# Latent projection in one piece, even maxima turned behind it, one softmax exponential and the value copies behind a group's exponentials, six steps moved

## What is computed

```python
# causal self-attention, 32 query heads, 8 key heads, head width 16
q = (x @ wq).reshape(b, s, NH, HD); k = (x @ wk)...; v = (x @ wv)...
attn = softmax(where(causal, q k^T * HD**-0.5, min))     # 56 x 56 for a head
x = x + (attn v) @ wo
# cross-attention over 1500 context rows, in a latent space of 32
C_q = Q @ Wq_d                                   # Q = layernorm(x)
C_kv = K @ Wkv_d                                 # the latents: 1500 x 32 for an element
scores = (C_q @ W_qk) C_kv^T / sqrt(LKV)         # 16 heads x 56 rows x 1500
out = softmax(scores) @ (C_kv @ Wv_u)
x = x + out
# feed-forward with a LoRA term
x = x + layernorm(x) @ kernel + bias + LoRA
```

## Time and profile before

| | |
|---|---|
| median of 3 executions | 644.15 us |
| profiled execution, its own time | 645.84 us |
| its span, first to last instruction | 644.0 us |
| PE matmul busy | 584.1 us, 91% |
| DVE busy | 432.5 us, 67% |
| POOL busy | 412.7 us, 64% |
| ACT busy | 302.1 us, 47% |
| granted TensorE clock, mean | 0.968 |

### The profile page before, as it was taken

The page is one execution under the profiler, slowest core; times in us unless marked ns, Lnnn a source line. Parts: engine busy times, 40 slices in busy tenths (PEclk is TensorE's granted clock), DMA queues, the critical chain, the costliest instruction groups (busy, mean ns, idle before and its releaser), DMA issues.

```text
span 644.0 us, 11508 instructions
## 1 busy us (share of the span) xinstructions
PE 584.1 (91%) x4164; PEld 315.5 (49%) x4164; DVE 432.5 (67%) x715; ACT 302.1 (47%) x642; POOL 412.7 (64%) x385
## 2 busy tenths in 40 slices
PE   7889797998999899999999899998999899988887
PEld 7436353455446354545446355455446355434445
DVE  2737964678757967778747957678757967656632
ACT  1421434537444555437444555437444555464460
POOL 5002166598758887598758887588758887789000
PEclk9997788899999999999999999999999999999899
DMA  9959511651048110751039110761039110200000
GB/s 320 409 107 348 208 36 24 251 206 35 12 120 317 59 45 22 268 204 39 9 108 336 52 45 22 253 219 32 16 93 334 68 45 23 64 19 0 24 2 15
DMA packets 31578, 77.40 MB, mean 120 GB/s; under 512 B 11297, under 2 KB 24961, under 8 KB 29218
## 3 DMA queue, kind: packets, MB, share of 16 engines
q1 hardware_dynamic: 30854, 75.27, 34.9%
q10 hardware_dynamic: 668, 1.40, 0.6%
HBM read 58.92 MB, written 2.88 MB: 96 GB/s over the span
## 4 chain that ended last, share of the span: by engine, by line
PE 58%; DVE 19%; ACT 6%; POOL 4%; SPq 4%; issue 4%; DMA 4%; ACTq 0%; POOLq 0%; DVEq 0%
PE st_ps L711 11%; PE mx_ps L754 9%; PE pv_ps L726 8%; PE mi_ps L496 4%; PE mi_ps L490 4%; DVE mx_p L1143 4%; POOL acc L1214 3%; PE mi_ps L503 3%; DVE p L1066 2%; PE mi_ps L586 2%; SPq L402 2%; DMA ctx_sb<-in_ctx_t 2%; DVE xn L1018 2%; PE mi_ps L590 2%; DVE p L1107 2%
## 5 line engine op out<-in xcount | busy, mean ns | idle before, releaser
L1214 POOL TENSOR_TENSOR acc<-acc,p_ring 125x448 f32<-125x448 f32 x290 | 348.0, 1200 | 65.4 <-ACT p_ring L941 25.8
L1143 DVE TENSOR_REDUCE mx_p<-mx_ps 128x1 f32<-128x500 f32 x336 | 210.0, 669 | 98.9 <-PE mx_ps L754 97.9
L941 ACT ACTIVATE p_ring<-st_ps 125x448 f32<-125x448 f32 x372 | 183.4, 544 | 151.6 <-PE st_ps L711 139.7
L711 PE MATMUL st_ps<-q_st,c_st 98*125 98x448 f32 x372 | 146.3, 432 | 9.8 <-ACT p_ring L941 8.6
L754 PE MATMUL mx_ps<-c_st,q_st 96*128 96x500 f32 x336 | 142.1, 457 | 12.2 <-DVE mx_p L1143 5.1
L711 PEld LDWEIGHTS st_ps<-q_st,c_st 98*125 98x125 f32 x372 | 65.3, 190 | 99.3 <-ACT p_ring L941 79.9
L726 PE MATMUL pv_ps<-p_ring,c_nat 125*32 125x448 f32 x768 | 94.5, 564 | 1.9 <-ACT ox L840 1.0
L754 PEld LDWEIGHTS mx_ps<-c_st,q_st 96*128 96x128 f32 x336 | 63.6, 197 | 43.7 <-DVE mx_p L1143 17.6
L1222 POOL TENSOR_TENSOR rstd<-mv,eps_col 128x1 f32<-128x1 f32 x24 | 4.6, 190 | 117.1 <-DVE mv L1014 116.6
L503 PE MATMUL mi_ps<-ctx_sb,wkv_sb 128*32 128x375 f32 x480 | 46.8, 511 | 5.5 <-DVE p L1066 5.5
L1214 POOL TENSOR_TENSOR acc<-p_ring 125x448 f32<-125x448 f32 x29 | 35.6, 1226 | 19.2 <-ACT p_ring L941 19.2
(11 more groups left out here) (137 smaller groups left out, 677.9 us busy)
## 6 DMA issues: line engine op xcount, KB each, us to landing
ctx_sb<-in_ctx_t SPq DMA_DIRECT2D x16, 3000.0 KB, 11.6
c_st<-ct_hl SPq DMA_DIRECT2D x192, 46.9 KB, 2.3
q_st<-q_hl SPq DMA_DIRECT2D x90, 56.0 KB, 2.0
x_sb<-in_x SPq DMA_DIRECT2D x8, 256.0 KB, 2.8
out_y<-x3n SPq DMA_DIRECT2D x16, 112.0 KB
wq_sb<-in_wq SPq DMA_DIRECT2D x2, 512.0 KB, 6.4
kern_sb<-in_lora_a SPq DMA_DIRECT2D x1, 1024.0 KB, 14.2
wo_sb<-in_wo SPq DMA_DIRECT2D x1, 1024.0 KB, 17.6
```

Source lines behind the costliest of these rows:

```text
L711: mm(st_bank(unit)[0:KC, 0:HALF], c_st[:, b % 4, t * KT + k * KC:t * KT + (k + 1) * KC], q_st[:, b // 2 % 2, b % 2, half * HALF:(half + 1) ...
L941: act.activation(p_ring[:, unit % PR, :], st_bank(unit)[0:KC, 0:HALF], ACT.Exp, scale=float(L) ** -0.5).then_inc(exp_done, 1)
L1143: ve.tensor_reduce(mx_p[:, p:p + 1], mx_ps[unit % MXB][:, 0:KP], AX.X, ALU.max).then_inc(red_done, 1)
L1214: po.tensor_tensor(dst, first, p_ring[:, unit % PR, :].rearrange("p (h s) -> p h s", s=S), ALU.add).then_inc(acc_done, 1)
```

## The change

```diff
-PIECES_IN = [3, 2, 4, 0, 0, 0, 0, 3, 4, 0, 3, 0]
+PIECES_IN = [3, 2, 4, 0, 0, 0, 0, 3, 4, 0, 2, 0]
-FIRST_PIECES_IN = [3, 2, 4, 0, 0, 0, 2, 4, 4, 0, 0, 0]
+FIRST_PIECES_IN = [3, 2, 4, 0, 0, 0, 1, 4, 4, 0, 0, 0]

 STEPS = [
-    [("Ah", "a"), ("M", 2), ("L0", "n"), ("M", 1), ("A", "a"), ("AS", "a"), ("N0", "n")],
+    [("L0", "n"), ("Ah", "a"), ("A", "a"), ("M", 2), ("N0", "n"), ("M", 1), ("AS", "a")],
     [("CT", "a"), ("M", 1), ("T1", "n")],
     [("K", "n"), ("M", 1), ("Qh", "n"), ("M", 3), ("Q1", "n")],
-    [("WA", "n"), ("M", 1), ("SA", "n"), ("M", 2), ("WB", "n"), ("M", 1), ("NM", "m"), ("SB", "n"), ("SM0", "n"),
+    [("WA", "n"), ("M", 2), ("SA", "n"), ("M", 1), ("WB", "n"), ("M", 1), ("SB", "n"), ("NM", "m"), ("SM0", "n"),
      ("SM1", "n")],
-    [("SE0", "n"), ("Ah", "b"), ("MT", "m"), ("A", "b"), ("SE1", "n"), ("V", "n"), ("SN0", "n")],
-    [("CT", "b"), ("SN1", "n"), ("AS", "b")],
+    [("SE0", "n"), ("Ah", "b"), ("MT", "m"), ("A", "b"), ("V", "n"), ("SN0", "n")],
+    [("SE1", "n"), ("VC", "n"), ("CT", "b"), ("SN1", "n"), ("AS", "b")],
     [("P0", "n"), ("M", 1), ("P1", "n"), ("M", 1), ("P2", "n"), ("P3", "n"), ("XC", "f"), ("M", 1)],
-    [("O1", "n"), ("M", 3), ("Y", "f")],
+    [("O1", "n"), ("Y", "f"), ("M", 3)],
     [("DN", "f"), ("Wh", "n"), ("M", 1), ("W1", "n"), ("M", 1), ("DT", "f"), ("N1", "n")],
-    [("YT", "f"), ("M", 1), ("T2", "n"), ("M", 1), ("CQ", "n"), ("M", 1), ("H", "n"), ("N2", "f")],
+    [("YT", "f"), ("M", 1), ("T2", "n"), ("M", 2), ("CQ", "n"), ("M", 1), ("H", "n"), ("N2", "f")],
...
-BANK = {"Ah": (1, 0), "A": (1, 0), "CT": (1, 0), "MT": (0, 1), ...
+BANK = {"Ah": (1, 0), "A": (1, 0), "CT": (1, 0), "MT": 1, ...
+LATE_SUMS = (0, 8)

# TensorE
+            def turn_maxima(b):
+                pe.wait_ge(nm_step, 3 * b + 3)
+                pe.transpose(step_bank("MT", b)[0:2 * ROWT, KG * 128:(KG + 1) * 128],
+                             nm_hl[:, :, :].rearrange("p a j -> p (a j)").bitcast(F32), ident[:, :])\
+                    .then_inc(ps["MT"], 1)
 # V
-                        pe.wait_ge(mt_sb, 2 * n - 1)
+                        pe.wait_ge(s1_sb, 4 * n + 4)
 # A
-                    last = latents(o, slot, (2, 3))
+                    latents(o, slot, (2, 3)).then_inc(ps[name], 1)
+                    if n % 2 == 0 and n > 0:
+                        turn_maxima(n - 2)
+                    return
 # MT
                     if n % 2 == 0 and n + 2 < B:
-                        pe.wait_ge(s1_sb, 2 * n + 7)
+                        return
                     if n == B - 2:
-                        pe.wait_ge(ct_sb, B)
+                        pe.wait_ge(f2_sb, n // 2 - 1)
...
+                    turn_maxima(n)
 # sums, in the group's loop over t
-                        if t == 1 and 0 <= bl < B:
+                        if t == (3 if g in LATE_SUMS and bm < B else 1) and 0 <= bl < B:
                             sums(bl, gl)

# ScalarE: the step VC makes the copies of V; the copy of the maxima reads the new columns
-                    copy(m_t[:, :], o[0:2 * ROWT, 0:128]).then_inc(mt_sb, 1)
+                    copy(m_t[:, :], o[0:2 * ROWT, KG * 128:(KG + 1) * 128]).then_inc(mt_sb, 1)
...
+                    behind = "P1" if g == GROUPS and i + 1 < PAIRS else None
-                    if 0 <= bl < B and gl % KG == KG - 1:
+                    if 0 <= bl < B and gl % KG == KG - 1 and not behind:
                         out_of_sums(bl, gl // KG)
                     for name, n in steps_of(i, g):
                         step(name, n, i, g)
+                        if name == behind and 0 <= bl < B:
+                            out_of_sums(bl, gl // KG)
```

More of the change, by code:

```diff
@@ L99 @@
 ]
-BANK = {"Ah": (1, 0), "A": (1, 0), "CT": (1, 0), "MT": (0, 1), "T1": 1, "K": 1, "Qh": 0, "Q1": 0,
+BANK = {"Ah": (1, 0), "A": (1, 0), "CT": (1, 0), "MT": 1, "T1": 1, "K": 1, "Qh": 0, "Q1": 0,
         "SA": (0, 1), "SB": (0, 1), "V": 0, "P0": 1, "P1": 0, "P2": 1, "P3": 0, "O1": 0, "Y": 1,
@@ L630, in step @@
                     if n % 2 == 0 and n + 2 < B:
-                        pe.wait_ge(s1_sb, 2 * n + 7)
+                        return
                     if n == B - 2:
-                        pe.wait_ge(ct_sb, B)
+                        pe.wait_ge(f2_sb, n // 2 - 1)
                     if n % 2 and n + 1 < B:
                         pe.wait_ge(qh_lo, n // 2 + 2)
-                    pe.wait_ge(nm_step, 3 * n + 3)
-                    last = pe.transpose(o[0:2 * ROWT, 0:128],
-                                        nm_hl[:, :, :].rearrange("p a j -> p (a j)").bitcast(F32), ident[:, :])
+                    turn_maxima(n)
+                    return
                 elif name == "Y":
@@ L642, in step @@
                         pe.wait_ge(f2_sb, n)
+                    if n + 2 == PAIRS:
+                        pe.wait_ge(mt_sb, B - 1)
                     pe.wait_ge(ox_sb, 4 * n + 4)
@@ L672, in step @@
                 elif name == "T3":
-                    if n + 2 == PAIRS:
-                        pe.wait_ge(mt_sb, B - 1)
                     pe.wait_ge(ln[2], 5 * n + 5)
@@ L850, in step @@
                     return
-                if name not in ("T1", "V", "Q1", "P0", "P1", "P2", "P3", "SE0", "SE1", "O1", "T2", "CQ", "H", "A",
+                if name not in ("T1", "VC", "Q1", "P0", "P1", "P2", "P3", "SE0", "SE1", "O1", "T2", "CQ", "H", "A",
                                 "CT", "MT", "Y", "DN", "T3", "F1"):
@@ L860, in step @@
                     return
+                name = "V" if name == "VC" else name
                 o = step_bank(name, n)
@@ L963, in _ @@
             act.wait_ge(dve_c, 2)
-            for name in ("V", "SE0", "A", "SE1", "CT", "P0", "P1"):
+            for name in ("VC", "SE0", "A", "SE1", "CT", "P0", "P1"):
                 step(name, 0)
```

## The result

The changed kernel takes 680.1 us (median of 4, 673.06 to 682.25) against 644.6 us before. The ratio is 1.054, with a 95% interval of 1.0492 to 1.0587: slower by 5.4%. The prediction was 667 us, with a range from 648 to 680. The direction and the two main waits were right. The size was short by 13 us, so that the result lies at the very end of the range, which I had drawn that far for the clock. The runs show that most of what was missing is the clock and some 3 us are longer waits.

A forecast was written before the change was run, and what follows sets the result against it. TensorE sets the pace (58% of the chain, DVE 19%). Terms of 1.1 + 2.2 + 0.3 = 3.6 us a body, times 6 = 21.6, on a median of 644.15 gave 667 us with one microsecond for the clock; range 648 to 680.

The forecast's parts named there:

- the two main waits: PE waiting for DVE's reductions twice a body: about 2.2 us at piece 9 in g2, 1.1 behind CQ in g9.
- Group 9: T2's second piece in g9: piece 18 waits for piece 15's reduction behind YT, +1.1 us a body, bounds +0.5 and +1.5.
- Groups 0 to 2: L0 first and AS last in g0: PE waits at piece 9, +2.2 us a body, bounds 0.45 and 2.7.
- the meeting with POOL: In g0, N0 waits for POOL's first add and AS costs 2.1 us; with no meeting, PE's wait is 0.45.
- Groups 3 to 8: Waits removed there are mostly replaced by others: +0.3 us a body, bounds -2.3 and +1.0.
- The gain before V: Time saved in groups 3 to 8 up to the scores of g6: 1.0 us a body.
- the piece ahead of SA: Its reduction stands ahead of SA's mask adds, for which WB waits: +0.3 us a body.
- the maxima's DMA has slack: The maxima's transpose and DMAs come 1.3 us later, but are needed only in g6, over 5 us on.
- The sum: 1.1 + 2.2 + 0.3 = 3.6 us a body, times 6 = 21.6 us.
- The clock: Rival, chance 0.13: each body's new 2 us pause brings a clock dip, +10 us, 677; the forecast itself left one microsecond.

The follow-up runs named there:

- u_g9: The changed kernel with the maxima piece behind T2 in group 9 put back to group 10: 666.87 us, ratio 1.0335 to the kernel before.
- b_g9: The kernel before with only the one maxima piece of group 10 moved behind T2 in group 9: 655.94 us, ratio 1.0212.
- gains: The kernel before with only those parts of the change that take waits away at no known cost: 647.58 us, ratio 1.0062.
- small adds: Both kernels with POOL's adds cut to 56 of their 448 columns: 638.81 us for the changed kernel, 623.76 for the one before.
- the control: The kernel before with POOL's adds cut to 56 of their 448 columns: 623.76 us.
- fill: The changed kernel with ten unread matmuls in each of three waits of PE, in bodies 1 to 6: 677.74 us, ratio 1.0543.

## Why the prediction was right, and where it was short

**Group 9.** Forecast +1.1 us a body, from piece 18 waiting for 15. Measured +1.17 in Wh to H, and the row with 1.12 us. Right, and shown from both sides by u_g9 and b_g9. H to F2 kept its length, so that nothing further on returned any of it.

**Groups 0 to 2.** Forecast +2.2, bounds 0.45 and 2.7. Measured in F2 to K, on average over the five bodies: +2.06, and by the clock in none of them. With x at its old place of body 2 (L0 6.64 us after the start of F2's last part), the 9.47 us from L0 to K make it 16.1 against 13.8, +2.3. With small adds the same count gives 14.4, +0.6, for which I had 0.45. So 1.7 us are the meeting with POOL and the rest the order on DVE, much as forecast, and AS took 0.70 + 1.44 = 2.14 us for my 2.1. What I had wrong is the place: 0.65 us are lost at piece 6 already and only 1.33 at piece 9. That the two engines take turns shows in the rows at 302.37 and 303.49. The Trainium skill (SBUF — State Buffer, section "SBUF: two separate sides") states one exclusive lock, which whichever of the two starts first holds for the whole instruction. These rows agree with it.

**Groups 3 to 8.** Forecast +0.3, measured in stretches without a fall: K to V -1.0, V to O1 +1.8, O1 to Wh +0.2, together +1.0 (0.92 on average). The gain before V came out at the 1.0 us that the prediction carried on, though its own items add up to only 0.6: in gains K to V is 16.20, 1.2 less than before, and the piece ahead of SA then costs 0.2 of it, not 0.3. The term was short by what follows V. With small adds V to O1 is 12.54, as in the control, so that its 1.8 us are the meeting with POOL: SN's two products take 0.8 us longer each, and I had taken them at their old length. POOL's adds now run where it was waiting before, and AS of g5 starts 8.25 us after V does, where it started 5.66 after it before. That the maxima's DMA has slack was wrong too: the first score of g6 waits 0.3 us for it.

**The sum.** Without the clock, 1.16 + 2.06 + 0.92 = 4.14 us a body, against 3.6 forecast. Times six that is 3 us of the 13 missing, and groups 3 to 8 are where they come from.

**The clock** was the term that failed: "leaving one microsecond for the clock". Over the five bodies it took 10.4 us, and 1.1 in the kernel before. I had it as a rival with a chance of 0.13 and +10 us, which is nearly what came, on the evidence of a single fall in body 3. The trace held more: before body 1, where DVE lags, the clock fell five times, each time next to a wait of PE of 1.6 to 2.1 us. A forecast that puts two new waits of 1 to 2 us into each body should have taken this for the likeliest case. How often it would fall couldn't be read off: in the changed kernel only nine falls came behind 21 waits of over 1 us.

## What to carry to other kernels

Count how far each engine may run ahead of the next (here three banks) at each place of an order written by hand, before moving a piece into a place where an engine waits: the wait may be there because the next engine is busy, and the fourth piece then stops everything behind it. Removing small waits ahead of one that another engine sets only adds them up there. A wait of over a microsecond on TensorE is to be priced with the half clock that can follow it (here 10 us in all). Where it can't be removed, a few idle matmuls that fit into it are worth a try: they gave the changed kernel those 10 us back, and the kernel before 2 to 3. Made too many, they cost as much as they give (fill).

## What was not expected of the hardware

The clock fell to half behind waits of 1.1 to 1.4 us: nine times in the changed kernel between 118 and 560 us, each time behind such a wait (306.0, behind one of 0.3 and one of 1.25; 514.2, behind one of 1.16 alone). Twelve waits of the same size had no fall behind them, so the wait alone doesn't settle it; what does isn't shown. Small matmuls in the waits held the clock at full speed through all of bodies 1 to 6, in two runs, although PE's own work waited just as long for DVE.

Four groups of DVE's operations cost twice as much beside POOL's full adds as beside small ones (81.3 and 42.0 us). SM's differences (L1123), of the same kind and shape as one of them, kept their 1092 ns, and DVE's reductions too (L1131: 1076 and 1081 ns). With seven eighths of POOL's columns left out, the kernel before takes 623.8 us instead of 645.0, though POOL is on its chain with only 4%.
